# A pairwise-interaction tower on one Trainium2 core: tiles of 256, 256, 512, 512, 512 rows instead of four of 512, and 124 weight blocks instead of 128

## The reference, cut to what matters

```python
e = jnp.stack([tbl_f[ids[:, f]] for f in range(32)], axis=1)   # 2048 rows, 32 fields, 64 numbers
p, q = e[:, ids_x, :], e[:, ids_y, :]                          # the 496 pairs of fields x < y
z = jnp.einsum('bpj,bpj->bp', jnp.einsum('bpi,pij->bpj', p, w), q)
h = jnp.concatenate([z, dense_ctx], axis=1)                    # 496 + 16 = 512
h = jnp.maximum(h @ W_top1 + b_top1, 0.0)                      # 512 -> 512
h = jnp.maximum(h @ W_top2 + b_top2, 0.0)                      # 512 -> 256
y = h @ W_top3                                                 # 256 -> 1
```

## Time and profile before

| what | value |
|---|---|
| median of 3 runs | 858.94 us (858.76 to 859.58) |
| span of the profiled execution | 856.9 us |
| the profiled execution's own time | only its span is given; the median of the runs is 2.0 us above it |
| PE busy | 782.8 us, 91% |
| DVE busy | 592.4 us, 69% |
| POOL busy | 574.1 us, 67% |
| ACT busy | 195.7 us, 23% |
| mean granted clock of TensorE | 0.980 |

### The profile page before, as it was taken

One profiled execution on the slowest core, in us unless ns is written; L12 is line 12 of the kernel. 1 busy time (PEld: TensorE's weight loads), 2 busy tenths in 40 slices (PEclk: granted clock), 3 DMA queues, 4 the chain that ended last, 5 costly groups with the idle time before them and its releaser, 6 DMA issues.

```text
span 856.9 us, 10445 instructions
## 1 busy us (share of the span) xinstructions
PE 782.8 (91%) x3912; PEld 287.9 (34%) x3912; DVE 592.4 (69%) x512; ACT 195.7 (23%) x333; POOL 574.1 (67%) x597
## 2 busy tenths in 40 slices
PE   0467739998989999999999999999999999999998
PEld 0122213333333333333333333333333333333333
DVE  0145528977877768868689677877788677887750
ACT  1222202131222132311322222311322223200002
POOL 6777775778777777777787777777777777710100
PEclk9969969999999999999999999999999999999999
DMA  4524539969797887888697986888786988994820
GB/s 131 203 52 100 122 78 197 218 156 200 167 199 166 182 187 158 191 181 173 152 203 157 204 182 139 196 184 182 140 204 161 200 195 189 193 187 92 167 56 0
DMA packets 38601, 138.07 MB, mean 161 GB/s; under 512 B 11092, under 2 KB 11476, under 8 KB 28056
## 3 DMA queue, kind: packets, MB, share of 16 engines
q0 software_dynamic: 28048, 101.75, 60.3%
q1 hardware_dynamic: 10504, 35.67, 12.2%
HBM read 52.43 MB, written 0.01 MB: 61 GB/s over the span
## 4 chain that ended last, share of the span: by engine, by line
PE 76%; POOL 13%; issue 5%; DMA 5%; DVE 1%; ACT 0%; POOLq 0%; DVEq 0%
PE main_ps L332 44%; PE z_ps L355 17%; POOL emb L233 12%; PE x_ps L386 8%; PE x_ps L312 4%; DMA prod<-prod 4%; PE main_ps L386 2%; POOL prod L245 1%; DMA emb<-in_tbl,idx 1%; DVE prod L419 1%; PE main_ps L333 1%; ACT quad_t L442 0%; DMA idx<-in_ids 0%; ACT y_sb L465 0%; POOLq L230 0%
## 5 line engine op out<-in xcount | busy, mean ns | idle before, releaser
L419 DVE TENSOR_TENSOR prod<-main_ps,quad_t 128x1024 f32<-128x1024 f32 x448 | 521.8, 1217 | 151.8 <-PE main_ps L333 151.3
L233 POOL DMA_INDIRECT emb<-in_tbl,idx x512 | 494.0, 965 | 165.4 <-issue 149.2
L332 PE MATMUL main_ps<-e_t,w_sb 64*128 64x512 f32 x1024 | 488.6, 617 | 4.1 <-ACT e_t L431 4.1
L333 PE MATMUL main_ps<-e_t,w_sb 64*128 64x512 f32 x1024 | 488.6, 617 | 0.0
L332 PEld LDWEIGHTS main_ps<-e_t,w_sb 64*128 64x128 f32 x1024 | 185.0, 191 | 260.8 <-issue 184.3
L355 PE MATMUL z_ps<-prod,const_sb 128*32 128x512 f32 x1400 | 177.4, 604 | 28.3 <-DMA prod<-prod 26.1
L333 PEld LDWEIGHTS main_ps<-e_t,w_sb 64*128 64x128 f32 x1024 | 185.0, 191 | 0.0
L419 DVE TENSOR_TENSOR prod<-main_ps,e_t 128x1024 f32<-128x1024 f32 x64 | 78.1, 1220 | 83.8 <-PE main_ps L333 83.8
L442 ACT ACTIVATE quad_t<-x_ps 32x512 f32<-32x512 f32 x224 | 131.2, 586 | 2.7
L245 POOL DMA_DIRECT2D prod<-prod x81 | 80.0, 993 | 74.0 <-DVE prod L419 69.3
L431 ACT ACTIVATE e_t<-x_ps 128x512 f32<-128x512 f32 x64 | 38.2, 597 | 400.0 <-PE x_ps L312 400.0
(11 more groups left out here) (11 smaller groups left out, 24.3 us busy)
## 6 DMA issues: line engine op xcount, KB each, us to landing
prod<-prod POOLq DMA_DIRECT2D x81, 1024.0 KB
w_sb<-in_w SPq DMA_DIRECT2D x65, 512.0 KB, 5.8
emb<-in_tbl,idx POOLq DMA_INDIRECT x512
w_sb<-in_w SPq DMA_DIRECT2D x1, 1024.0 KB, 11.9
z_sb<-in_ctx SPq DMA_DIRECT2D x64, 2.0 KB
idx<-in_ids SPq DMA_DIRECT2D x1, 192.0 KB, 9.6
const_sb<-in_const SPq DMA_DIRECT2D x1, 125.0 KB, 2.2
idx<-in_ids SPq DMA_DIRECT2D x1, 64.0 KB, 1.9
```

The costliest lines, as they stand in the source:

```text
L233: pool.indirect_dma_start(out=emb[:, n % G_SLOTS, s, odd * EMBED:(odd + 1) * EMBED], out_offset=None, in_=tables[f], in_offset=bass.Indire ...
L332: nc.tensor.matmul(main_ps[:, slot, :], w_sb[LOW, u % W_SLOTS, :], even[LOW, 0, :], start=True, stop=True)
L333: nc.tensor.matmul(main_ps[:, slot + 1, :], w_sb[UP, u % W_SLOTS, :], odd[UP, 0, :], start=True, stop=True)\
L419: nc.vector.tensor_tensor(prod[:, s:s + 2, :], main_ps[:, slot:slot + 2, :], e_q, ALU.mult)\
```

## The change

- **Tiles.** Five tiles of 256, 256, 512, 512 and 512 rows. A duo of a narrow tile has 4 gathers and 2 transposes. A round of a narrow tile holds two groups of weight blocks; one step (three fit into main_ps, as units did) holds two units side by side in the column halves of the same two banks, four matmuls of 256 columns, and DVE multiplies both in one instruction. A narrow tile has 16 rounds, and all weights are loaded once more, five times in all.
- **The quads' own products.** The pairs of fields inside two quads took 4 units before (a duo's two, two times, shared over rounds); now a "star" group of 3 units makes the 12 pairs of two quads. A full tile has 28 groups of 4 and 4 groups of 3 units: 124 instead of 128. The stars read rearranged copies of duos that ACT makes (mix_quad: 4 copies for each quad).
- **Folds.** 71 rounds are folded instead of 81: none of the 32 rounds of the narrow tiles, 25, 24 and 22 of the 32 of tiles 2, 3 and 4.
- **Order.** The duos' places in a full tile are those of STEADY, the MLP steps' those of MLP_AT. Gathers: in the first 32 rounds (both narrow tiles) POOL may run up to 6 duos ahead; from then on only until 172 + 4 x (rounds since) gathers are out, and what a duo still lacks is issued at the duo's own place in the list. POOL no longer waits for products at the end of a round that isn't folded.
- **Others.** W_top1's rows stand in another order for narrow tiles, so w1 is loaded twice; one DMA carries two rows of dense_ctx.

Along the new list, in rounds of tile 3 (tile 4 has the same; tile 2 from its duo 10 on): the duo of number j is transposed before round R, and its last gathers stand at the end of round e, or (j = 7) at its own place in the list.

| j | 4 | 5 | 6 | 7 | 8 | 9 | 10 | 11 | 12 | 13 | 14 | 15 |
|---|---|---|---|---|---|---|---|---|---|---|---|---|
| R | 0 | 2 | 3 | 4 | 7 | 9 | 11 | 13 | 15 | 18 | 20 | 22 |
| e | -2 | 0 | 2 | own place | 6 | 8 | 10 | 12 | 14 | 16 | 18 | 20 |

Rounds 2, 7, 18, 29 (stars) and 6, 14, 22, 28 of tile 3 are not folded. In tile 0 duo 8 is transposed before step 15, duo 9 before step 19.

```diff
-TILE = 512
-TILES = BATCH // TILE
-SUBS = TILE // P
+FULL, HALF = 512, 256
+WIDTHS = (HALF, HALF, FULL, FULL, FULL)
+TILES = len(WIDTHS)
+FIRST_COL = [sum(WIDTHS[:t]) for t in range(TILES)]
...
-def ahead(n):
-    return 2 if n < 10 else 3 if n < DUOS else G_SLOTS
...
+def order_groups():
+    low = []
+    for m in range(13, 1, -1):
+        low += [(m, q) for q in range(QUADS - 1, m // 2, -1)]
+    low += [(m, q) for q in range(QUADS - 1, 0, -1) for m in (1, 0)]
+    groups = [("low", low[k:k + 2]) for k in range(0, len(low), 2)]
+    for at, q in ((2, 7), (7, 5), (18, 3), (29, 1)):
+        groups.insert(at, ("star", (q, q - 1)))
+    return groups
+
+
+GROUPS = order_groups()
+NGROUP = len(GROUPS)
+SLOTS4 = 4
...
+def steps_of(t, r):
+
+    if WIDTHS[t] == FULL:
+        return [(r, (p,)) for p in range(4 if GROUPS[r][0] == "low" else 3)]
+    return [(g, (j, j + 2) if GROUPS[g][0] == "low" or j == 0 else (j,)) for g in (2 * r, 2 * r + 1) for j in range(2)]
...
-FOLDS = [(t, r) for t in range(TILES) for r in FULL if (t == TILES - 1 or r not in (9, 17, 25, 29)) and (t < TILES - 1 or r < ROUNDS - 3)]
-POOL_GATHERS = 4
+def foldable(t, r):
+    return all(GROUPS[g][0] == "low" for g in groups_of(t, r))
+
+
+UNFOLDED = {0: range(16), 1: range(16), 2: range(4), 3: (6, 14, 22, 28), 4: (6, 14, 22, 28, 30, 31)}
+FOLDS = [(t, r) for t, r in ROUNDS if foldable(t, r) and r not in UNFOLDED[t]]
...
-DUO_ROUNDS = (-9, -7, -5, -3, -1, 1, 3, 5, 7, 9, 11, 13, 15, 17, 19, 21)
-MLP_ROUNDS = (6, 10, 14, 18, 22, 26, 30)
+STEADY = (-6, -4, -3, -1, 0, 2, 3, 4, 7, 9, 11, 13, 15, 18, 20, 22)
+DUO_AT = {1: (-4, -3, -2, -1, -1, 0, 1, 2, 3, 4, 5, 6, 7, 8, 9, 10), 2: STEADY, 3: STEADY, 4: STEADY}
+MLP_AT = {1: (4, 5, 7, 9, 11, 12, 13)} | {t: (5, 9, 13, 17, 21, 25, 29) for t in (2, 3, 4)}
...
+            n = max(FIRST_DUO[t][m] - 1, 0) if t == 0 else min(STEP0[ROUND0[t] + DUO_AT[t][j]], FIRST_DUO[t][m])
+            at[m] = max(n, at.get(m + 1, 0))
+            put(at[m], ("duo", t, m))
+        for q in range(QUADS - 1, -1, -1):
+            g = STAR_GROUP[q if q % 2 else q + 1]
+            star = g if WIDTHS[t] == FULL else g // 2
+            lead = (2 if WIDTHS[t] == FULL else 0) + q % 2
+            put(max(STEP0[max(ROUND0[t] + star - lead, 0)], at[2 * q]), ("mix", t, q))
         if t:
-            for n, r in enumerate(MLP_ROUNDS):
-                due.setdefault(t * NUNIT + ROUND * r, []).append(("mlp", t - 1, n))
+            for n, r in enumerate(MLP_AT[t]):
+                put(STEP0[ROUND0[t] + r], ("mlp", t - 1, n))
...
+FREE_ROUNDS, FREE_GATHERS = 32, 172
...
-                if n >= ahead(n) and k == 0:
-
-                    pool.wait_ge(transposed, n - ahead(n) + 1)
+                if n >= G_SLOTS and k == 0:
+
+                    pool.wait_ge(transposed, n - G_SLOTS + 1)
...
-            todo = [(n, k) for n in range(TILES * DUOS) for k in range(2 * SUBS)]
-            seen = 0
-            for kind, t, n in EVENTS:
+            todo = [(n, k) for n in range(TILES * DUOS) for k in range(gathers(n // DUOS))]
+            total, seen = len(todo), 0
+            for kind, a, b in EVENTS:
                 if kind == "duo":
-                    seen = duo_number(t, n) + 1
-                elif kind == "unit" and n % ROUND == ROUND - 1:
-                    paced = t > 0 or n > 10 * ROUND
-                    room = len([g for g in todo if g[0] < seen + ahead(g[0])])
-                    for _ in range(min(room, POOL_GATHERS) if paced else room):
+                    while todo and todo[0][0] <= duo_number(a, b):
                         gather(*todo.pop(0))
-                    if (t, n // ROUND) in FOLDS:
-                        fold(t, n // ROUND)
-                    elif paced:
-
-                        pool.wait_ge(products, NUNIT * t + n + 1)
-                        pool.nop(nofuse=True)
+                    seen = duo_number(a, b) + 1
+                elif kind == "end":
+                    goal = total if a < FREE_ROUNDS else min(total, FREE_GATHERS + 4 * (a + 1 - FREE_ROUNDS))
+                    while total - len(todo) < goal and todo[0][0] < seen + G_SLOTS:
+                        gather(*todo.pop(0))
+                    if ROUNDS[a] in FOLDS:
+                        fold(a)
...
+                slot = 2 * (n % MAIN)
+                for h, p in enumerate(ps):
+                    kind, what = GROUPS[g]
+                    u = (NGROUP * SLOTS4 * t + SLOTS4 * g + p) % W_SLOTS
+                    if kind == "low":
+                        low = up = what[p % 2][0]
+                    else:
+                        low, up = (side[0] // 2 for side in star_units(*what)[p])
+                    c = slice(HALF * h, HALF * h + WIDTHS[t])
+                    nc.tensor.matmul(main_ps[:, slot, c], w_sb[LOW, u, :], e_duo(t, low)[LOW, :], start=True, stop=True)
+                    last = nc.tensor.matmul(main_ps[:, slot + 1, c], w_sb[UP, u, :], e_duo(t, up)[UP, :], start=True, stop=True)
+                last.then_inc(mains, 1)
...
+                kinds = [GROUPS[g][0] for g in groups_of(t, r)]
+                if len(set(kinds)) == 1:
+                    spans = [(kinds[0], slice(0, FULL))]
+                else:
+                    spans = [(kind, slice(HALF * c, HALF * c + HALF)) for c, kind in enumerate(kinds)]
+                todo = []
+                for p in range(2 if folded else 4):
+                    for kind, c in spans:
+                        if kind == "low" or p < 3:
+                            todo += [(p, x, kind, c) for x in range(2)]
...
+                if kind == "star":
+                    if ps[0] == 0:
+                        dve.wait_ge(mixed, MIXED["mix", t, what[1]])
+                    for h, p in enumerate(ps):
+                        c = slice(HALF * (g % 2), HALF * (g % 2) + HALF) if WIDTHS[t] == HALF else slice(0, FULL)
+                        a = prod_tile(G, p, 0)
+                        ins = nc.vector.tensor_tensor(prod[:, a:a + 2, c], main_ps[:, slot:slot + 2, HALF * h:HALF * h + WIDTHS[t]],
+                                                      star_operand(t, *what, p), ALU.mult)
...
+            def mix_quad(t, q):
+                first, pair = q % 2 == 1, q if q % 2 else q + 1
+                act.wait_ge(evicted, EVICTED["duo", t, 2 * q])
+
+                if pair < QUADS - 1:
+                    act.wait_ge(products, FINAL_STAR[t][pair + 2] + 1)
+                elif t:
+                    act.wait_ge(products, FINAL_STAR[t - 1][1] + 1)
+                a, b = e_duo(t, 2 * q), e_duo(t, 2 * q + 1)
+                one, other = (mix(t, 0), mix(t, 3)) if first else (mix(t, 1), mix(t, 2))
+                nc.scalar.activation(one[LOW, :], a[LOW, :], ACT.Copy)
+                nc.scalar.activation(one[UP, :], b[UP, :], ACT.Copy)
+                if first:
+                    nc.scalar.activation(other[LOW, :], a[LOW, :], ACT.Copy)
+                    last = nc.scalar.activation(other[UP, :], b[LOW, :], ACT.Copy)
+                else:
+                    nc.scalar.activation(other[LOW, :], a[UP, :], ACT.Copy)
+                    last = nc.scalar.activation(other[UP, :], b[UP, :], ACT.Copy)
+                last.then_inc(mixed, 1)
```

More of the change, by code:

```diff
@@ L16 @@
 MLP_STEPS = HID1 // P + HID2 // P + 1
[L17 to L22 removed]
 def pair_index(i, j):
+    i, j = min(i, j), max(i, j)
     return i * (FIELDS - 1) - i * (i - 1) // 2 + j - i - 1
[L33 to L40, removed]
@@ new lines, with sources @@
+ROUND0 = [sum(rounds_of(k) for k in range(t)) for t in range(TILES + 1)]
+ROUNDS = [(t, r) for t in range(TILES) for r in range(rounds_of(t))]
+STEP0 = [0]
+for _t, _r in ROUNDS:
+    STEP0.append(STEP0[-1] + len(steps_of(_t, _r)))
+STEPS = [(g, k) for g, (t, r) in enumerate(ROUNDS) for k in range(len(steps_of(t, r)))]
+ROUNDS_KT = 8
+Z_TILES = [rounds_of(t) // ROUNDS_KT for t in range(TILES)]
+Z0 = [sum(Z_TILES[:t]) for t in range(TILES + 1)]
+def sources(g, p):
+    kind, what = GROUPS[g]
+    if kind == "low":
+        return (what[p % 2][0],)
+    return tuple(side[0] // 2 for side in star_units(*what)[p])
@@ L69 @@
+STAR_GROUP = {what[0]: g for g, (kind, what) in enumerate(GROUPS) if kind == "star"}
+FINAL_STAR = [{q: max(n for n, g, ps in tile_steps(t) if g == STAR_GROUP[q]) for q in STAR_GROUP} for t in range(TILES)]
 W_SLOTS, W_PART = 64, 8
 W_PARTS = W_SLOTS // W_PART
+PARTS_TILE = NGROUP * SLOTS4 // W_PART
 MAIN = 3
-P_SLOTS = 16
+P_ROUNDS = 4
 PAST = 3
-LAG = 4
-E_SLOTS = 8
+E_SLOTS, MIX_SLOTS = 8, 4
 Q_SLOTS = 8
 G_SLOTS = 6
-FULL = [r for r in range(ROUNDS) if all(PIECES[2 * r + h][0] == "low" for h in range(2))]
@@ L139, in order_events @@
-    ev += [("reduce", TILES - 1, ROUNDS - k) for k in range(PAST, 0, -1)] + [("z", TILES - 1, KTILES - 1)]
+    for G, (t, r) in enumerate(ROUNDS):
+        for k in range(len(steps_of(t, r))):
+            ev += due.get(STEP0[G] + k, [])
+            ev.append(("step", G, k))
+        ev.append(("end", G, 0))
+        if G >= PAST:
```

(29 more changed lines are left out.)

472 lines of the change are left out of this document (267 added, 205 removed).

## The result

| | before | after |
|---|---|---|
| median of 4 runs each | 858.96 us | 993.57 us (992.67 to 995.8) |
| span of the profiled execution | 856.9 us | 990.9 us |
| mean granted clock | 0.980 | 0.922 |
| PE busy | 782.8 us, 91% | 825.3 us, 83% |

After to before is 1.157, 95% interval 1.155 to 1.159. That PE is busier in us than before isn't more work: a slow clock stretches what it does.

A forecast was written before the change was run, and what follows sets the result against it. PE bounds the steady part, POOL's gathers the beginning. Start and work 799.7, x_ps 31, late gathers 88 and clock 21 give 940 us of span, so 942 us; range 885 to 978.

The forecast's parts named there:

- waits for x_ps in full tiles: Full tiles: six MLP steps behind duos each wait 3.1 us for ACT (18.6), plus 2 x 0.8 for transposes behind steps.
- late gathers: Tiles 2 to 4: duos' last gathers stand behind a fold waiting for products; PE waits 35.8, 35.8 and 15.9, sum 88 us.
- the upper bound: 978 us: clock falls at six 3.1 us waits (10), narrow slots take 0.25 (17), POOL itself late at folds (7).
- T + 11.2: Middle duos: gathers landed 11.2 us after T, the end on PE of the matmuls the last fold ahead waits for.
- POOL can't catch up: Full tiles: between late duos POOL gains no lead, as each new fold ties it to DVE, thus to PE.
- The clock: PE behind long waits: lower clock level for a while, 1.64 us lost at each of thirteen waits over 4.47 us, 21 us.
- my prices: PE times read from the profile before: MLP step 3.63 us, half-width 1.91, main round 3.64, folded reduce 1.00, duo's transposes 0.59.
- the likeliest case: Whole kernel as summed: 942 us, in the band 905 to 978, chance 62%.
- the thirteen: Waits forecast to exceed 4.47 us, the only ones charged with a slow clock, 21 us together.
- The start: Tile 0: gathers bound PE until duo 8 arrives at 50.1 us; loss at the start falls from 89 to 34 us.
- The other side: Rival, whole kernel: gathers aren't late, only start and x_ps count; 833 us, faster by 3%; chance 9%.

The follow-up runs named there:

- Both: Changed kernel with FREE_GATHERS' second number 188 instead of 172 and MLP steps kept apart from duos: 843.28 us, 0.981 of before.
- Gathers further ahead: Changed kernel with FREE_GATHERS' second number 188 instead of 172, so full tiles' gathers stand four rounds earlier in the list: 868.25 us, 1.013 of before.
- the kernel before with meetings: Kernel before the change with MLP steps before rounds 5, 9, 13, 17, 21, 25, 29, many right behind a duo: 919.69 us, 1.071 of before.

## Why the direction was right and the size wrong

The sum's terms against the trace, in us of span. Work behind the start is what it takes in "Both", less its waits; the clock is what is left of the span:

| term | forecast | measured |
|---|---|---|
| to duo 4 of tile 2 (round 32) | 242 | 252.5 |
| work behind it | 568.5 | 573.4 |
| waits for x_ps in full tiles | 20.2 | 19.1 |
| late gathers | 88 | 94.9 |
| waits for folds and for DVE | 0 | 3.0 |
| clock | 21 | 45.6 |
| a wait for dense_ctx in the tail | 0 | 2.4 |
| sum | 940 | 991 |

- **Late gathers:** right in size, and in mechanism for 72.2 of the 94.9 us. In tile 3 37.5 us instead of 35.8, in tile 4 37.9, in tile 2 19 instead of 15.9. The waits went with more lead; those behind a waiting fold went, but for 9.5 us, with the folds; and moving the gathers made such waits anew in the kernel before. Another 21.3 us (duos 5 and 6, and 14 of tile 2) come from POOL's own pace with the DMA engines full, which the sum put at nothing and only the upper bound had (7 us). Errors cancel: duos 5 and 14 were missed (4.9, 2.2 and 2.8), duo 6's number fits by luck, and at duo 7 the gathers landed 0.7 us sooner than T + 11.2.
- **"POOL can't catch up":** right that it doesn't; but in tiles 3 and 4 POOL is tied to DVE only from round 3 on. Ahead of that its own pace keeps it behind. The 16 gathers more of lead, once given, hold to the end.
- **x_ps:** right, 2.96 us each.
- **The clock:** here the prediction failed. "Thirteen of the waits are over 4.47 us: 21 us" took the 1.64 us behind one wait as the price of each, and counted none shorter than the one that I had seen lower the clock, though the rows left open all between 2.09 and 4.47 us. In the changed kernel all six waits of 2.96 us for ACT lower the clock, too. PE's timeline shows one of them:

```profile
551.96 5.40 PE L533 MATMUL x_ps<-z_sb,w_sb 128*128 128x512 f32 x8 [2.96 <-ACT quad_t L608]
```

  The six steps behind them take 3.59, 3.53 (half width, 1.91 by my prices), 5.33, 5.88, 5.33 and 5.92 us (3.63): 11.2 us lost. Behind the gather waits the starts give the price one by one. Sixteen of them, of 3.7 us and more, lose 31.8 us, 2.0 each, 1.7 to 3.1 where no MLP step follows at once. The two of 2.21 and 2.78 us lose nothing. A wait of 1.8 us for a fold at 458.62 with one of 0.4 behind it loses 1.6, and the 2.4 us for dense_ctx in the tail 1.7. That is 46.3 us, close to the 45.6 of the table. So of the 25 us missing 11.2 are the six (my upper bound had 10 for them and the likeliest case nothing), 5.9 three gather waits more than the thirteen, 4.6 the higher price of the thirteen, 3.3 the two short ones. With this term right the sum is 964 us of span, inside the range.
- **The start:** 10.5 us too early. Its mechanism is right (gathers until 50 us, then PE), and so are the waits for x_ps (11.0 us). The causes of the 10.5 weren't tried one by one. The trace shows 3.7 by duo 8, with a clock of 0.70 between 40 and 50 us; behind it one wait of 2.8 us for DVE at 143.46, and a clock of 0.83 from 120 to 130 and from 140 to 150 us. So part of this is the clock as well.
- **The other side** (833 if gathers aren't late): tried by "Gathers further ahead", and even then the kernel isn't faster than before: 868. Of the 35 us between, start and work are 15, waits for folds 10.6 and the clock behind the waits for ACT over 7 (five of six steps slow). That rival's number was too low for some of the same reasons as mine.

## What to carry to other kernels

In a queue walked in order, a transfer is as late as the last waiting instruction ahead of it: count an item's lead from the last wait in its queue, not in rounds. Then count the queue's own pace too: here four gathers and a fold take 6.15 us against PE's 4.6, so the lead shrinks with every folded round and gives out first in the tightest cluster of consumers. Price a wait of 3 us or more on TensorE, in a kernel like this one, as the wait plus about 2 us of slow clock. And try a pacing constant before judging a new tiling: here one number decided between 16% slower and 1% slower, and one more line of places made it 2% faster.

## What the runs showed that I had not expected

- The clock falls already behind 2.96 us of idle time (up to 3.16 in the kernel before with meetings), in 6 of 6 cases of the changed kernel, 5 of 6 with gathers further ahead and 10 of 12 of the kernel before with meetings. Below that the length of the wait alone doesn't decide. In the changed kernel the clock holds behind 2.78 us and falls behind 2.44 (the tail takes 15.5 us to its next part, with gathers further ahead 13.8); in "Both" it holds behind 2.54 and falls behind 2.31. PE's timeline of the changed kernel behind the 2.78, with the transposes at their usual 0.59:

```profile
397.34 0.66 PE L437 MATMUL x_ps<-const_sb,emb 128*128 128x128 f32 x4 [2.78 <-DMA emb<-in_tbl,idx]
397.93 0.69 PE L466 MATMUL main_ps<-e_t,w_sb 64*128 64x512 f32 x1
```

- The loss hardly grows with the wait: 2.5 us behind 9.40, 3.1 behind 4.46, 1.7 behind 3.71.
- Filling idle time on TensorE keeps the clock up (0.922 to 0.970) and brings little where the next wait is for the same late producer.
- How long a gather takes to land depends on what POOL did before. Behind a fold that had waited, the transposes follow 2.9 to 4.3 us after the last gather's start (2.54 in the earlier trace rows), so the fold's own megabyte hardly holds it up; where POOL issues without a stop, 4.5 to 6.1 us. Whether that is the DMA engines, 0.98 busy there, or POOL's queue no run separates.
